# A convolution and deformable-sampling kernel: merged transfers on SyncE, and a denser table of taps and groups

## The chip, the cores and the metric

The kernel runs on one core of one Trainium2 chip. The metric is the device time of one execution in microseconds (us). The engines are TensorE (PE in the profile, PEld its weight loads), VectorE (DVE), ScalarE (ACT), GpSimd (POOL) and SyncE (SP), which here issues nearly all DMAs; 16 DMA engines move the bytes. Most executions agree within 0.3%.

## The reference, cut to what matters

```
x = x + _L0_conv_ref(_gn(x), ...)     # 14 convolutions and 2 upsamplings on (2, 64, 128, 128)
x = x + _L1_conv_ref(_gn(x), w_off, b_off, w_def)

offsets = conv3x3(x, w_off) + b_off   # 18 channels: dy, dx of 9 taps
val     = sum over 4 corners of x at (y + ky + dy, x + kx + dx), bilinear weights
out     = einsum('bckhw,ock->bohw', val, w_def)
```

The second line is a deformable convolution: for each pixel and each of nine taps it takes a value between pixels at a place that the offsets give, and weighs the values with a 64 x 64 matrix for each tap.

## The kernel before

**The stages.** Image 0 and then image 1 pass through the convolutions (until about 355 us and 737 us). After each, in the stage that I call *offsets*, TensorE computes the 18 offset channels, POOL splits them in three bfloat16 parts (`offp`), the normalised pixels are turned (`turned`), and SP stores both to DRAM: `store_parts` writes `offd`, one transfer for each of 8 tiles, `store_pixels` writes `pixd`. During image 0's offsets stage ACT's own queue loads image 1 into `xm`, and DVE takes its statistics as it comes. From about 780 us the *sampling* stage works on both images together, in 32 strips of four rows (`STRIPS`).

**A strip.** One strip needs windows of pixels (`win`, 12 transfers, `load_windows`), offsets (`offs`, for four strips at once, `load_offs`), and the first sum x1 (`x1t`, `load_x1`), and it stores its result (`store_strip`). All of them stand in SP's one queue, in this order for strip s: wait until all groups of s are sampled, load the windows of s+2, wait for the result of s, store it, load the x1 of s+2. After every fourth strip stands one `load_offs`.

**The units of a step.** In the step of strip s each engine goes through nine units, n = 0 to 8, always in program order. In unit n TensorE makes the distances of tap n of strip s+1 (`distances`, 8 matmuls, into one of two PSUM slots, so it needs the `absolute` of two units ago), ACT takes their absolute value (`absolute`), and DVE makes hat functions and products (`hats`, then `product` of the tap before). Behind that stand by tables:

- `WEIGHED_AT`: `weigh` of the last strip's taps on TensorE. The first of them waits until ACT has copied all six groups of that strip, with the two copies of columns at the edges that follow group 5.
- `GROUPS_AT`: `sample_group` on TensorE, a set of blocks of this strip (24 matmuls for groups 0 to 3 and 16 for 4 and 5, twice that in the trace since an f32 matmul stands there as two), and the copy of it out of PSUM, on ACT for groups 0, 1, 3, 4, 5 and on DVE for group 2. Group g uses the PSUM banks of group g-2, and waits for its copy.
- `RESULT_AT`: DVE adds the weighed sum and x1 (`strip_result`), before the `hats` of that unit. Group 1 uses the same banks as the sum, so it waits for this addition.

The waits that matter, in the code:

```
    if g >= 2:
        pe.wait_ge(*group_taken(s, g - 2))
...
        else:
            pe.wait_ge(strip_sum, s)
...
    pe.wait_ge(vals_act, (len(ACT_GROUPS) + 1) * (s + 1))
```

Strips 0 to 3 and the last four stand unrolled on TensorE; the others run in a loop.

Of the kernel before, what the change touches and what calls it, by code (L numbers as in the profile page):

```python
# [23 lines left out]
PS = 4  # L24
# [70 lines left out]
OFF_LOADS = 16 * 2 * PARTS * IMAGES  # L95
# [76 lines left out]
def build(nc, x, w4, w3, wds, wdec, woff, boff, wdef, wtaps, gmat, ident, sel, rampc, selg, places, out):  # L172
    es = ExitStack()
    with es:
# [233 lines left out]
        offd = nc.dram_tensor("offd", [IMAGES, ODD_AT, STRIPS + 2, PARTS * 2 * PS * HALF_W], BF16, kind="Internal").ap()  # L408
# [49 lines left out]
        def margins(eng):  # L458

            n = 0  # L460
            for b in range(IMAGES):
# [7 lines left out]
                for strip in (0, STRIPS + 1):  # L469
                    eng.dma_start(offd[b, 0:OFFC, strip, :], zeros_b[0:OFFC]).then_inc(pads_in, 16)  # L470
# [48 lines left out]
        def _(sp):  # L519
# [23 lines left out]
            def store_parts(b, n):  # L543

                sp.wait_ge(off_split, b * 8 + (n + 1 + SLOTS))
                batch, loc = divmod(n, 2)
                first = 1 + 8 * (2 * (batch // 2) + loc) + 4 * (batch % 2)
                dst = offd[bass.ds(b, 1), :, first:first + 4, :].rearrange("b c s n -> (b s) c n")
                sp.dma_start(dst, offp[:, n % SLOTS].rearrange("c p n -> c (p n)")).then_inc(parts_out[n % SLOTS], 16)
# [19 lines left out]
            def load_offs(q, slot):  # L569

                for b in range(IMAGES):
                    for h in range(2):
                        for part in range(PARTS):
                            lo = (2 * part + h) * PS * HALF_W
                            src = offd[b, 0:OFFC, bass.ds(QUAD * q, QUAD + 2), lo:lo + PS * HALF_W]
                            at = CH * h + OFFC * part
                            dst = offs[at:at + OFFC, slot, b].rearrange("c (s n) -> c s n", s=QUAD + 2)
                            sp.dma_start(dst, src).then_inc(offs_in[slot], 16)
# [12 lines left out]
            def strip_rows(d, t, j, two):  # L591

                return d[:, :, bass.ds(2 * PS * t + (PS * j + 2 * two - 1), 2), :].rearrange("b c i w -> b c (i w)")

            def load_x1(t, j):

                for two in range(2):
                    for b in range(IMAGES):
                        dst = x1t[CH * two:CH * two + CH, j, b]
                        if isinstance(t, int) and t == 0 and j == 0 and two == 0:  # L600
                            first = x1d[b, :, 0, :]
                            src = bass.AP(first.tensor, first.offset, [[H0 * W0, CH], [0, 2], [1, W0]])
                            sp.dma_start(dst.rearrange("c (i w) -> c i w", w=W0), src).then_inc(x1_in[j], 16)
                        else:
                            sp.dma_start(dst, strip_rows(x1d, t, j, two)[b]).then_inc(x1_in[j], 16)

            def store_strip(t, j):
                sp.wait_ge(strip_sum, 2 * t + (j + 1))
                for two in range(2):
                    for b in range(IMAGES):  # L610
                        src = outt[CH * two:CH * two + CH, j, b]
                        if isinstance(t, int) and t == 0 and j == 0 and two == 0:
                            sp.dma_start(out[b, :, 0, :], src[:, W0:2 * W0]).then_inc(out_done[j], 16)
                        else:
                            sp.dma_start(strip_rows(out, t, j, two)[b], src).then_inc(out_done[j], 16)
# [7 lines left out]
            def first_strips(b):  # L623
# [7 lines left out]
                for i in range(SLOTS):  # L631
                    sp.wait_ge(parts_out[i], MARGIN + (b * 32 + 16))
# [8 lines left out]
                load_offs(1, 1)  # L641

# [73 lines left out]
            for i in range(SLOTS):  # L716
                sp.wait_ge(pm_out[i], MARGIN + (IMAGES * 2 * 64))
                sp.wait_ge(parts_out[i], MARGIN + (IMAGES * 2 * 16))
# [7 lines left out]

            for j in range(2):
                load_x1(0, j)
# [16 lines left out]
            with sp.Fori(0, STRIPS // 8 - 1) as h:  # L745
                load_offs(2 * h + 2, 0)
                strip_pair(4 * h + 2)
# [1391 lines left out]
```

## Time and profile before

| | us |
|---|---|
| median of 3 runs | 1370.67 (1370.42 to 1372.49) |
| the profiled execution, its own time | 1373.18 |
| its span, first to last instruction | 1371.4 |

| engine | busy us, share of the span |
|---|---|
| PE | 1072.0, 78% |
| DVE | 886.0, 65% |
| ACT | 668.6, 49% |
| POOL | 62.2, 5% |

A load of x1 (64 KB) lands 2.2 us after its issue (median, the page's list of DMA issues).

The profile does not count the issuing of DMAs as busy, so SP has no line there: its queue is read in the timeline. Shares are means over stages with different limits.

### The profile page before, as it was taken

The page shows a single profiled execution, that of the slowest core. Times are in us where ns is not written, and L with a number is a line of the kernel's source. Part 1 is how long each engine was busy: PE and PEld are TensorE (multiplying, and loading weights), DVE is VectorE, ACT ScalarE, POOL GpSimd, SP SyncE. Part 2 cuts the span into 40 slices and gives each one's busy share as a digit, 9 for nine tenths or more (in the row PEclk, how much of TensorE's full clock was granted, in tenths as well). Part 3 has the DMA queues.
Part 4 walks back from the last instruction along what each step waited for, and adds up shares of the span by engine and source line. Part 5 has one row for each costly group of instructions (what it writes and reads, how often), then busy time and mean ns, then how long its engine had stood idle before and what let it go on. Part 6 is the DMA issues. An engine that isn't in the chain of part 4 may idle for free.

```text
span 1371.4 us, 42739 instructions
## 1 busy us (share of the span) xinstructions
PE 1072.0 (78%) x17334; PEld 675.1 (49%) x17334; DVE 886.0 (65%) x1379; ACT 668.6 (49%) x901; POOL 62.2 (5%) x87
## 2 busy tenths in 40 slices
PE   0799999975836999999767675888786878687875
PEld 0243346752312333467533254677565666566664
DVE  4878751527938777624279475888676867686870
ACT  0533433003444324330033774887776867586871
POOL 0000000000240000000002600000000000000000
PEclk9999999998877999999998778999999999898998
DMA  9000022204570000222034453433333333333341
GB/s 187 1 1 2 2 89 64 64 2 115 122 204 24 1 1 1 89 63 64 2 83 102 127 136 105 118 109 108 112 106 101 107 108 109 92 111 106 110 117 41
DMA packets 94709, 109.87 MB, mean 80 GB/s; under 512 B 12607, under 2 KB 81855, under 8 KB 92856
## 3 DMA queue, kind: packets, MB, share of 16 engines
q1 hardware_dynamic: 86056, 101.74, 27.6%
q10 hardware_dynamic: 8464, 5.37, 1.7%
q8 instruction: 147, 2.41, 0.8%
q14 instruction: 42, 0.34, 0.1%
HBM read 74.85 MB, written 32.22 MB: 78 GB/s over the span
## 4 chain that ended last, share of the span: by engine, by line
issue 47%; PE 38%; DVE 5%; ACT 3%; DMA 2%; POOL 2%; SPq 1%; ACTq 0%; POOLq 0%; DVEq 0%
PE psum L838 21%; PE psum L907 12%; DMA xm<-x 2%; PE psum L971 2%; DVE v L1632 1%; PE psum L948 1%; SPq L528 1%; POOL offr L2009 1%; POOL offp L2013 1%; ACT xm L1383 1%; PE psum L929 1%; DVE xm L1798 1%; PE psum L938 1%; DVE stats L1801 0%; PE psum L985 0%
## 5 line engine op out<-in xcount | busy, mean ns | idle before, releaser
L838 PE MATMUL psum<-v,u 64*64 64x512 f32 x3072 | 337.9, 597 | 17.9 <-DVE v L1632 12.7
L1455 ACT ACTIVATE dist<-psum 128x1024 f32<-128x1024 f32 x288 | 288.9, 1025 | 53.3 <-PE psum L1034 43.7
L1845 DVE TENSOR_SCALAR dist<-dist 128x1024 f32<-128x1024 f32 x288 | 198.2, 689 | 120.3 <-ACT dist L1455 119.7
L1081 PE MATMUL psum<-hat,win 64*64 64x144 f32 x4096 | 207.6, 332 | 86.7 <-DMA win<-pixd 45.5
L838 PEld LDWEIGHTS psum<-v,u 64*64 64x64 f32 x3072 | 133.3, 134 | 220.9 <-issue 220.5
L1081 PEld LDWEIGHTS psum<-hat,win 64*64 64x64 f32 x4096 | 160.3, 145 | 121.0 <-issue 119.0
L1855 DVE TENSOR_TENSOR hat<-dist 128x512 f32<-128x512 f32 x288 | 194.4, 684 | 0.3
L1458 ACT ACTIVATE val<-psum 128x864 f32<-128x864 f32 (+3 forms) x230 | 146.9, 676 | 94.8 <-PE psum L1081 87.1
L1154 PE MATMUL psum<-val,wdefs 64*64 64x256 f32 x1944 | 164.7, 394 | 32.5 <-ACT val L1458 24.2
L1034 PE MATMUL psum<-offs,sels 61*64 61x256 bf16 x2304 | 138.8, 287 | 19.7 <-issue 11.7
L1154 PEld LDWEIGHTS psum<-val,wdefs 64*64 64x64 f32 x1944 | 91.5, 137 | 46.3 <-issue 42.9
L1034 PEld LDWEIGHTS psum<-offs,sels 61*64 61x64 bf16 x2304 | 91.5, 113 | 34.4 <-issue 31.9
L1632 DVE TENSOR_TENSOR v<-stage 128x1024 f32<-128x1024 f32 x64 | 75.1, 1220 | 20.7 <-ACT stage L1334 20.7
L971 PE MATMUL psum<-tm,woffs 64*32 64x512 f32 x1152 | 70.4, 628 | 11.8 <-DVE tm L1749 11.8
L1632 DVE TENSOR_TENSOR v<-xm 128x1024 f32<-128x1024 f32 (+1 forms) x64 | 73.6, 1221 | 5.7 <-ACT xm L1342 4.1
L1325 ACT ACTIVATE mid<-psum 128x1024 f32<-128x1024 f32 x32 | 32.7, 1022 | 86.4 <-PE psum L838 86.4
L1342 ACT ACTIVATE xm<-xm 128x2048 f32<-128x2048 f32 x16 | 30.8, 1922 | 82.7 <-DVE xm L1682 82.7
L955 PE MATMUL psum<-gn,gmats 128*128 128x1 f32 x16 | 4.7, 362 | 80.2 <-DVE gn L1592 77.4
L1672 DVE TENSOR_TENSOR psum<-mid,psum 128x1024 f32<-128x1024 f32 x32 | 39.6, 1237 | 42.0 <-ACT mid L1325 42.0
L907 PE MATMUL psum<-htm,w3s 64*64 64x256 f32 x1152 | 63.0, 375 | 0.0
L1573 DVE SCALAR_TENSOR_TENSOR hxm<-psum,hxm 128x256 f32<-128x256 f32 x32 | 13.6, 424 | 73.7 <-PE psum L907 73.4
L1334 ACT ACTIVATE stage<-psum 128x1024 f32<-128x1024 f32 x32 | 36.4, 1143 | 47.0 <-PE psum L838 47.0
(144 smaller groups left out, 1094.8 us busy)
## 6 DMA issues: line engine op xcount, KB each, us to landing
win<-pixd SPq DMA_DIRECT2D x256, 68.0 KB
win<-pixd SPq DMA_DIRECT2D x128, 136.0 KB
raw<-x SPq DMA_DIRECT2D x16, 512.0 KB, 7.6
x1d<-xm SPq DMA_DIRECT2D x16, 512.0 KB, 6.0
pixd<-turned SPq DMA_DIRECT2D x64, 128.0 KB, 5.0
x1t<-x1d SPq DMA_DIRECT2D x128, 64.0 KB, 2.2
out<-outt SPq DMA_DIRECT2D x126, 64.0 KB, 2.1
offd<-offp SPq DMA_DIRECT2D x16, 384.0 KB
```

Source lines behind the costliest of these rows:

```text
L838: mm = pe.matmul(o, u4[half, i, v, ky, :], V[half, at:at + CHUNK, cg, v, :], start=start, stop=stop, skip_group_check=True)
L907: mm = pe.matmul(by_rows(o, level), w3s[CH * rg:CH * rg + CH, W_AT[layer], tap, :], rows_in(src, level, stride, rg, slot, step, tap), star ...
L971: mm = pe.matmul(by_rows(o, FULL), woffs[CH * rg:CH * rg + CH, tap, :], rows_in(T, FULL, 1, rg, slot, 4 * half + j, tap), start=tap == 0, ...
L1034: mm = pe.matmul(dst, sels[of, 2 * n + axis, :], offs[of, slot, b, lo:lo + PS * HALF_W], start=True, stop=True, skip_group_check=True)
L1081: mm = pe.matmul(dst[:, :, :, q:q + PS], win[half, j, b, block_ + h, :], rows, start=True, stop=True, skip_group_check=True)
L1154: mm = pe.matmul(dst.rearrange("c (r w) -> c r w", w=W0), w, val[half, slot, r0:r0 + 2, cols], start=k == 0, stop=k == TAPS - 1, skip_grou ...
L1455: act.activation(dist_at(j, n), psum[:, slot:slot + 2, :], ACT.Abs).then_inc(dist_abs, 1)
L1458: return act.activation(dst, src, ACT.Copy)
L1632: dve.tensor_tensor(dst, a, c, op).then_inc(v_made[v], 1)
L1672: dve.tensor_tensor(pair_banks(n, True), m2, m3, ALU.subtract).then_inc(minus_made, 1)
L1845: dve.tensor_scalar(d, d, 1.0, 1.0, ALU.min, ALU.subtract).then_inc(hats_made, 1)
L1855: dve.tensor_tensor(to, d[:, :, 0:PS * HALF_W], d[:, :, PS * HALF_W:], ALU.mult).then_inc(prod_dve, 1)
```

## The change

1. `offd` is laid out with the part as a dimension of its own. `store_parts` writes a tile in three transfers (one for each part) where it wrote one; `load_offs` reads all three parts at once: 4 transfers where there were 12. The constant `sel` has its rows in the new order.
2. `load_x1` and `store_strip` move both images in one transfer: two each for a strip where there were four.
3. The x1 of strips 0 and 1 is loaded inside `first_strips`, before the last pixels are stored, and no longer at the start of the strip loop.
4. The tables: taps in units 0 to 2, three each; groups 0 to 5 in units 3 to 8, one each; the result in unit 3.

```
-WEIGHED_AT = {1: [0, 1], 2: [2, 3], 3: [4, 5], 4: [6, 7, 8]}
-GROUPS_AT = {5: [0], 6: [1, 2], 7: [3], 8: [4, 5]}
-RESULT_AT = 5
+WEIGHED_AT = {0: [0, 1, 2], 1: [3, 4, 5], 2: [6, 7, 8]}
+GROUPS_AT = {3: [0], 4: [1], 5: [2], 6: [3], 7: [4], 8: [5]}
+RESULT_AT = 3
...
-                sp.dma_start(dst, offp[:, n % SLOTS].rearrange("c p n -> c (p n)")).then_inc(parts_out[n % SLOTS], 16)
+                for part in range(PARTS):
+                    dst = offd[bass.ds(b, 1), :, part, first:first + 4, :].rearrange("b c s n -> (b s) c n")
+                    sp.dma_start(dst, offp[:, n % SLOTS, part]).then_inc(parts_out[n % SLOTS], 16)
...
-                        for part in range(PARTS):
-                            lo = (2 * part + h) * PS * HALF_W
-                            src = offd[b, 0:OFFC, bass.ds(QUAD * q, QUAD + 2), lo:lo + PS * HALF_W]
+                        src = offd[b, 0:OFFC, :, bass.ds(QUAD * q, QUAD + 2), PS * HALF_W * h:PS * HALF_W * (h + 1)]
+                        dst = offs[CH * h:CH * h + HALF_K, slot, b].rearrange("c (s n) -> c s n", s=QUAD + 2)
+                        sp.dma_start(dst, src.rearrange("c p s n -> (c p) s n")).then_inc(offs_in[slot], 16)
...
+                        sp.dma_start(dst, strip_rows(x1d, t, j, two)).then_inc(x1_in[j], 16)
...
+                        sp.dma_start(strip_rows(out, t, j, two), src).then_inc(out_done[j], 16)
...
                 load_offs(1, 1)
+                for j in range(2):
+                    load_x1(0, j)
```

How the instructions stand on three engines, before and now (a row names its line, the operation, what it writes and reads, and the shape; line numbers shift by six):

TensorE, the later part of one step of the loop, before. `psum<-offs,sels` are distances, `psum<-val,wdefs` taps (here 7 and 8, with the last of 6), `psum<-hat,win` groups:

```order
L1034 MATMUL psum<-offs,sels 64x256 x8
L1154 MATMUL psum<-val,wdefs 64x256 x12
L1034 MATMUL psum<-offs,sels 64x256 x8
L1081 MATMUL psum<-hat,win 64x36x4 x12
L1034 MATMUL psum<-offs,sels 64x256 x8
L1081 MATMUL psum<-hat,win 64x36x4 x24
L1034 MATMUL psum<-offs,sels 64x256 x8
L1081 MATMUL psum<-hat,win 64x36x4 x12
L1034 MATMUL psum<-offs,sels 64x256 x8
L1081 MATMUL psum<-hat,win 64x36x4 x16
L1093 MATMUL psum<-hat,win 64x12 x8
```

The same place now:

```order
L1148 MATMUL psum<-val,wdefs 64x256 x12
L1028 MATMUL psum<-offs,sels 64x256 x8
L1075 MATMUL psum<-hat,win 64x36x4 x12
L1028 MATMUL psum<-offs,sels 64x256 x8
L1075 MATMUL psum<-hat,win 64x36x4 x12
L1028 MATMUL psum<-offs,sels 64x256 x8
L1075 MATMUL psum<-hat,win 64x36x4 x12
L1028 MATMUL psum<-offs,sels 64x256 x8
L1075 MATMUL psum<-hat,win 64x36x4 x12
L1028 MATMUL psum<-offs,sels 64x256 x8
L1075 MATMUL psum<-hat,win 64x36x4 x8
L1028 MATMUL psum<-offs,sels 64x256 x8
```

A group now stands between each two distances, where groups 1 and 2 (x24) and groups 4 and 5 (x16) stood together; group 2 follows the distances of unit 5, not of unit 6, and the taps stand in front of three distances, not of four.

DVE, from the result to the copy of group 2, before (`dist<-dist` is `hats`, `hat<-dist` is `product`, the rows of registers are waits):

```order
L1881 TENSOR_TENSOR outt<-psum,x1t 128x512
L1843 REGISTER_ALU
L1845 TENSOR_SCALAR dist<-dist 128x1024
L1855 TENSOR_TENSOR hat<-dist 128x512
L1843 REGISTER_ALU
L1845 TENSOR_SCALAR dist<-dist 128x1024
L1855 TENSOR_TENSOR hat<-dist 128x512
L1873 REGISTER_ALU
L501 COPY val<-psum 128x2x36x12
```

The same two now:

```order
L1875 TENSOR_TENSOR outt<-psum,x1t 128x512
L1837 REGISTER_ALU
L1839 TENSOR_SCALAR dist<-dist 128x1024
L1849 TENSOR_TENSOR hat<-dist 128x512
L1837 REGISTER_ALU
L1839 TENSOR_SCALAR dist<-dist 128x1024
L1849 TENSOR_TENSOR hat<-dist 128x512
L1837 REGISTER_ALU
L1839 TENSOR_SCALAR dist<-dist 128x1024
L1849 TENSOR_TENSOR hat<-dist 128x512
L1867 REGISTER_ALU
L502 COPY val<-psum 128x2x36x12
```

The result stands two units earlier, the copy one unit earlier, so three units of hats and products lie between them where two did.

SP, from the second load of offsets to the strip loop, before:

```order
L578 DMA offs<-offd 18x6x256 x12
L560 DMA pixd<-turned 16x8x256 x8
L549 DMA offd<-offp 4x32x1536
L560 DMA pixd<-turned 16x8x256 x4
L549 DMA offd<-offp 4x32x1536
L560 DMA pixd<-turned 16x8x256 x4
L549 DMA offd<-offp 4x32x1536 x2
L603 DMA x1t<-x1d 64x2x128 x2
L605 DMA x1t<-x1d 64x256 x6
```

The same place now:

```order
L577 DMA offs<-offd 54x6x256 x4
L601 DMA x1t<-x1d 64x2x128 x2
L603 DMA x1t<-x1d 64x2x256 x3
L562 DMA pixd<-turned 16x8x256 x8
L551 DMA offd<-offp 4x32x512 x3
L562 DMA pixd<-turned 16x8x256 x4
L551 DMA offd<-offp 4x32x512 x3
L562 DMA pixd<-turned 16x8x256 x4
L551 DMA offd<-offp 4x32x512 x6
```

The loads of x1 have moved in front of the last stores of pixels and parts, and each store of parts is three.

## Rows read from the trace of the kernel before

**Rows 1.** Waits of TensorE, 859 to 1332 us: total us, times, longest
```profile
PE psum L1081 <- DMA win<-pixd: 45.5, 13, 10.1
```

**Rows 2.** Waits of SP's queue, the same stretch
```profile
SPq L589 <- PE psum L1081: 0.8, 1, 0.8
```

**Rows 3.** Timeline of SP: start us, us, what, how many
```profile
817.73 1.17 SPq L549 DMA_DIRECT2D offd<-offp  x2
831.30 1.40 SPq L603 DMA_DIRECT2D x1t<-x1d  x2
...
836.67 7.82 SPq L589 DMA_DIRECT2D win<-pixd  x12
...
892.22 6.10 SPq L578 DMA_DIRECT2D offs<-offd  x12
...
966.50 9.14 SPq L589 DMA_DIRECT2D win<-pixd  x12
975.75 2.49 SPq L615 DMA_DIRECT2D out<-outt  x4
978.44 3.13 SPq L605 DMA_DIRECT2D x1t<-x1d  x4
...
1031.58 6.96 SPq L578 DMA_DIRECT2D offs<-offd  x12
```

**Rows 4.** Issues of the x1 loads, ns min/median/max
```profile
L605 SPq DMA_DIRECT2D x1t<-x1d x126: 468/532/1736, 832.7 to 1337.6; - x126
...
L603 SPq DMA_DIRECT2D x1t<-x1d x2: 659/672/686, 831.3 to 832.0; - x2
```

**Rows 5.** Timeline of ACT: start, us, in brackets idle before
```profile
873.47 1.05 ACT L1458 ACTIVATE val<-psum 128x576 f32<-128x576 f32 x3
...
885.99 0.97 ACT L1458 ACTIVATE val<-psum 128x864 f32<-128x864 f32 x1 [0.15 <-PE psum L1081]
886.84 1.02 ACT L1455 ACTIVATE dist<-psum 128x1024 f32<-128x1024 f32 x1
887.74 1.66 ACT L1458 ACTIVATE val<-psum 128x576 f32<-128x576 f32 x4
...
1330.68 1.64 ACT L1458 ACTIVATE val<-psum 128x576 f32<-128x576 f32 x4
```

**Rows 6.** Timeline of TensorE in the same strip, and two later places
```profile
878.48 1.51 PE L1154 MATMUL psum<-val,wdefs 64*64 64x256 f32 x23
879.72 0.49 PE L1034 MATMUL psum<-offs,sels 61*64 61x256 bf16 x7
879.94 0.31 PE L1081 MATMUL psum<-hat,win 64*64 64x144 f32 x1
...
885.91 0.84 PE L1081 MATMUL psum<-hat,win 64*64 64x144 f32 x16
...
889.69 1.09 PE L1154 MATMUL psum<-val,wdefs 64*64 64x256 f32 x16 [0.24 <-ACT val L1458]
...
926.63 1.28 PE L1081 MATMUL psum<-hat,win 64*64 64x144 f32 x23 [2.00 <-DMA win<-pixd]
...
1006.04 1.96 PE L1154 MATMUL psum<-val,wdefs 64*64 64x256 f32 x16
```

**Rows 7.** Timeline of DVE in the same strip: the result, the copy of group 2
```profile
881.64 0.68 DVE L1881 TENSOR_TENSOR outt<-psum,x1t 128x512 f32<-128x512 f32 x1
...
884.65 1.05 DVE L501 COPY val<-psum 128x864 f32<-128x864 f32 x1
```

**Rows 8.** Waits of TensorE, 820 to 837 us
```profile
PE psum L1081 <- DVE outt L1881: 16.2, 1, 16.2
```

**Rows 9.** Stretches: PE, PEld, DVE, ACT, POOL busy, PE clock, DMA share, GB/s
```profile
820.00:830.00 10.00, 0.30 (x11) 0.03 (x2) 0.14 (x1) 2.01 (x3) 0.00 (x0) 0.78 0.25 89
...
928.02:931.43 3.41, 3.41 (x65) 3.38 (x60) 1.39 (x3) 2.77 (x3) 0.00 (x0) 0.50 0.31 78
```

**Rows 10.** Timeline of DVE at image 1's start: its last statistics
```profile
412.51 2.48 DVE L1812 BATCH_NORM_STATS2 stats<-xm 128x6 f32<-128x512 f32 x4 [10.45 <-DMA xm<-x]
```

More of the change, by code:

```diff
@@ L94 @@
 LAST_BANKS = (4, 5)
[L95 removed]
+OFF_LOADS = 16 * 2 * IMAGES
 HALF_STRIP = BANK // 2
@@ L469, in margins @@
                 for strip in (0, STRIPS + 1):
-                    eng.dma_start(offd[b, 0:OFFC, strip, :], zeros_b[0:OFFC]).then_inc(pads_in, 16)
+                    eng.dma_start(offd[b, 0:OFFC, :, strip, :], zeros_b[0:OFFC].rearrange("c (p n) -> c p n", n=BANK)
+                                  ).then_inc(pads_in, 16)
         def settled(eng):
@@ L591, in strip_rows @@
             def strip_rows(d, t, j, two):
-                return d[:, :, bass.ds(2 * PS * t + (PS * j + 2 * two - 1), 2), :].rearrange("b c i w -> b c (i w)")
+                return d[:, :, bass.ds(2 * PS * t + (PS * j + 2 * two - 1), 2), :].rearrange("b c i w -> c b (i w)")
             def load_x1(t, j):
                 for two in range(2):
[L598 to L605, printed above, removed]
+                    dst = x1t[CH * two:CH * two + CH, j]
+                    if isinstance(t, int) and t == 0 and j == 0 and two == 0:
+                        for i in range(2):
+                            first = x1d[:, :, 0, :].rearrange("b c w -> c b w")
+                            sp.dma_start(dst[:, :, W0 * i:W0 * (i + 1)], first).then_inc(x1_in[j], 16)
+                    else:
+                        sp.dma_start(dst, strip_rows(x1d, t, j, two)).then_inc(x1_in[j], 16)
             def store_strip(t, j):
@@ L609, in store_strip @@
                 for two in range(2):
[L610 to L615, printed above, removed]
+                    src = outt[CH * two:CH * two + CH, j]
+                    if isinstance(t, int) and t == 0 and j == 0 and two == 0:
+                        first = out[:, :, 0, :].rearrange("b c w -> c b w")
+                        sp.dma_start(first, src[:, :, W0:2 * W0]).then_inc(out_done[j], 16)
+                    else:
+                        sp.dma_start(strip_rows(out, t, j, two), src).then_inc(out_done[j], 16)
             def sampling_constants():
@@ L725, in _ @@
             sp.wait_ge(off_split, IMAGES * 8 + SLOTS)
-            for j in range(2):
-                load_x1(0, j)
             def strip_pair(t, more=True):
@@ L745, in _ @@
             with sp.Fori(0, STRIPS // 8 - 1) as h:
-                load_offs(2 * h + 2, 0)
-                strip_pair(4 * h + 2)
-                strip_pair(4 * h + 3)
-                load_offs(2 * h + 3, 1)
-                strip_pair(4 * h + 4)
-                strip_pair(4 * h + 5)
+                for slot in range(2):
+                    load_offs(2 * h + (2 + slot), slot)
+                    strip_pair(4 * h + (2 + 2 * slot))
+                    strip_pair(4 * h + (3 + 2 * slot))
             strip_pair(STRIPS // 2 - 2)
@@ L767, in g_unit @@
                     for h in range(2):
-                        lo = (2 * part + h) * PS * HALF_W
-                        src = offd[bass.ds(b, 1), 0:OFFC, bass.ds(2 * t + (opar + 1), 1), lo:lo + PS * HALF_W]
+                        src = offd[bass.ds(b, 1), 0:OFFC, part, bass.ds(2 * t + (opar + 1), 1), PS * HALF_W * h:PS * HALF_W * (h + 1)]
                         dst = g_offs[OFFC * part:OFFC * part + OFFC].rearrange("c (r h x) -> c r h x", h=2, x=HALF_W)[:, :, h, :]
@@ L1878, in strip_result @@
                 dve.wait_ge(strip_conv, 4 * (s + 1))
-                dve.wait_ge(x1_in[j], uses * 64)
-                dve.wait_ge(out_done[j], MARGIN + ((uses - 1) * 64))
+                dve.wait_ge(x1_in[j], uses * 32 + 16 * (1 - j))
+                dve.wait_ge(out_done[j], MARGIN + ((uses - 1) * 32))
                 dve.tensor_tensor(outt[:, j], psum[:, SUM_BANKS[0]:SUM_BANKS[1] + 1, 0:HALF_STRIP], x1t[:, j],
@@ L2038, in selectors @@
         for part in range(PARTS):
-            s[:, OFFC * part + 2 * k + 1, k, 0] = 1.0
-            s[:, OFFC * part + 2 * k, k, 1] = 1.0
+            s[:, PARTS * (2 * k + 1) + part, k, 0] = 1.0
+            s[:, PARTS * 2 * k + part, k, 1] = 1.0
         s[:, HALF_K + 1 + K + kx, k, 0] = 1.0
```

20 lines of the change are left out of this document (8 added, 12 removed).

## The prediction

> **What bounds the kernel now.** I read the busy shares first: no engine is full, so something makes them wait, and the question is what ends the wait in each stage. The change touches the offsets stages lightly and the sampling stage in each of its 32 steps, so I read the waits there. TensorE waits 45.5 us in 13 waits for windows [rows 1], and the other engines' waits hang on those. The windows are late because of the queue that issues them: SP waited for TensorE only 0.8 us in 473 us [rows 2]. It issues without a pause: 9.1 us for the windows, 2.5 for four stores, 3.1 for four x1 loads, and 6 to 7 for the twelve offset loads after every fourth strip [rows 3]. From one load of offsets at 892.22 to the second next at 1031.58 are 8 strips in 139.4 us, 17.4 each.
>
> Strip by strip the end of the last copies on ACT is the best mark (I call it T). It stands at 874.52 for strip 3 (873.47 + 1.05), at 889.40 for strip 4 (887.74 + 1.66) and at 1332.32 for strip 30 [rows 5]. Strip 4, in which no window was late, took 14.9; the 27 steps to strip 30 took 16.96 each. So some 2 us of a step are SP's.
>
> **Part 1, SP per strip.** Two stores and two x1 loads fall away, and 8 offset loads of 12. What a merged transfer costs to issue no row shows exactly. The nearest is the first x1 load: it carries two runs for each of 64 partitions and took 0.67 where the plain one took 0.53 [rows 4]. From below a merged one costs what one costs now (0.53), from above what both cost (1.06). I take 0.67, as its shape is nearest. Then stores and loads take 4 x (0.67 + 0.1 between two) = 3.1 where they took 5.6: 2.5 saved; the offsets 4 x 0.7 for 6.5, 0.9 a strip. SP falls from 17.4 to 14.0, at the lower end 13.4, at the upper 17.
>
> The Trainium skill (Perfetto Trace Analysis, DMA Instruction — HWDGE) says that the issue as profiled holds the making of all descriptors. By it a merged transfer could cost what both did, the upper end. The rows do not fit a plain proportion: double the runs cost 0.67 against 0.53.
>
> **Part 2, the step on the engines.** If SP needs 14.0 and the engines more, the engines set the step, and now by the new tables. I follow the chain from T, with these spacings: ACT goes on 0.90 after an absolute value, 0.85 after a copy of 864 columns and 0.6 after one of 576, and the last group with its edge copies takes 1.06 (887.74 + 0.6 to 889.40) [rows 5]; three taps take 1.30 and a block of distances 0.22 before the next can start, and its ACT work starts 0.5 after it; 16 group matmuls are done after 0.84, so 24 after about 1.15; taps start 0.3 after T [rows 6]. On DVE five instructions lie between 881.64 and 884.65, so 0.60 each, and group 2's copy is 1.05 [rows 7]. In us after T:
>
> - Taps 0 to 2 run from 0.3 to 1.6, then distances 1, absolute 1 at 2.1; taps 3 to 5, distances 2 at 3.1, absolute 2 at 3.6; taps 6 to 8, distances 3 at 4.65, absolute 3 at 5.15. Absolute 0 had stood ready since T. So ACT idles 2.6 here: three taps and distances (1.5) stand against one absolute (0.9) in each unit. Before, five absolutes stood beside the same taps.
> - DVE: hats 2 at 4.7 (when absolute 2 ends), product 1 at 5.3, result 5.9 to 6.6. Group 1 can only then be sampled, from 6.75. ACT copies group 0 at 6.1, absolute 4 at 6.95, group 1 at 7.95, absolute 5 at 8.8, absolute 6 at 9.7, group 3 at 10.6, absolute 7 at 11.5.
> - DVE again: hats 5 has to wait for absolute 5 (ends 9.85), product 4 at 10.5, copy of group 2 from 11.1 to 12.1. Group 4 uses its banks, and starts 0.2 later, as at 884.65 + 1.05 and 885.91: 12.3. **This is what is late next**: ACT is free at 12.35 but gets group 4 at 13.2, absolute 8 at 13.8, group 5 at 14.7, T at 15.8.
>
> The old tables by the same chain give 14.5, and 14.9 was measured for strip 4; I add the difference, 0.35. So the step becomes **16.15**: 0.8 less than the mean of 16.96, though 1.25 more than a step of the old order that no window holds up. I keep 15.5 (nothing added, a little slack that I overlook) and 16.9 for the range. Over 27 steps: 27 x 0.81 = **21.9 us** less.
>
> Windows for strip s+2 are asked for at the end of step s and needed 4.9 into step s+2: 21 us, against 9.1 of issue and about 2.4 to land. They stay hidden while SP's 14.0 is below the step, so the two units by which group 0 moves ahead cost nothing. The store waits for the result, now 6.6 after T, still inside the 9.1 of the windows ahead of it.
>
> **Part 3, the start of sampling.** Now strip 1's group 1 waits 16.2 us [rows 8]: the result of strip 0 wants x1, whose loads stand behind the last stores' landing and are issued at 831.30 [rows 3]. With the loads moved ahead this wait goes. What is late next is the windows of strip 2: SP waits until all parts have landed before the strip loop, and only then issues them. They were issued at 836.67, after 5.4 us of x1 loads; now right behind the landing. But the landing moves. While only parts move, 10 us long, the DMA share is 0.25 with 89 GB/s [rows 9]: four engines of 16. A store of parts (393 KB) costs them 4.4 us, the four last ones 17.7. Pieces of 1 KB where they were 3 KB make this dearer, I take 15% (0 to 40%), +2.7. SP reaches the stores about 0.8 earlier (8 offset loads fewer at 0.5, five x1 loads more at 0.67), and issues 8 more transfers of 0.58 [rows 3], hidden behind the four engines' backlog. The landing goes from 831.3 to 833, group 0 of strip 2 is sampled at 833 + 7.8 + 2.4 = 843.2, T of strip 2 is 10.9 later (15.8 - 4.9), and T of strip 3 at 870.3 or with a slow clock at first 870.7, against 874.5: **3.8 us** less. Of the 16.2 only this is left.
>
> The Trainium skill (DMA: Bandwidth & Descriptors, the section on a DMA's increment of 16) has the number of engines as the largest divisor up to 16 of both sides' outermost sizes, and the lowest-numbered ones. The outermost size is 4 before and after, so by it the three transfers share the same four engines; were it otherwise, this landing would come some 8 us earlier.
>
> **Part 4, between the images.** Image 1's last statistics wait 10.45 us for its load [rows 10], which ACT's queue had issued some 20 us before and which shares those four engines with the parts. Two things change: eight stores take 1.2 us more of SP each and 15% more of the four engines (later, up to +4), and a piece of x of 512 bytes waits behind pieces of 1 KB, not of 3 KB, where the two queues take turns (earlier, up to -10). No row tells which weighs more. I take **-4**.
>
> **Part 5, the rest.** The last strip and the closing 39 us stay, within 1.
>
> **Sum.** 1373.18 (the profiled execution's own time, 2.5 over the median) - 21.9 - 3.8 - 4 = 1343.5, less 2.5: **1341 us**.
>
> **The rivals.**
>
> - *The clock falls in the new gaps* (slower). TensorE now idles about 1.8 twice in a step: before group 4 and before the taps, with 2 us of work between. For it: after a gap of 2.00 that ends at 926.63 [rows 6] the clock stood at 0.5, its lower level of 1.2 GHz, from 928.02 for 3.4 us [rows 9]; against it: before strip 4's taps 1.1 us did nothing. At that level 16 tap matmuls took 1.96 where they took 1.09 [rows 6], so a low stretch on the taps costs 1.7 a step; in each step that is 27 x 1.7 = 46, and 1341 + 46 = 1387. It decides from 17.2 a step on, two steps in three.
> - *The engines are not as far behind as the chain says*: the step comes down to the 14.9 of strip 4. 27 x 2.06 = 56 in place of 21.9: 1307. For it: the load of each unit is more even than before; against it: two waits of the chain (1.50 for each absolute beside three taps, group 2's copy) follow from program order.
> - *SP gets no shorter*, since a merged transfer costs what its parts did (the upper end): steps of 16.9, and only 3.8 and 4 are won: 1363. Were the start not won either, 1371, no change.
>
> **How the numbers follow.** The forecast 0.60 (1321 to 1360 with steps of 15.5 to 16.7 and the parts 3 and 4 at their ends); the clock 0.14; 14.9 a step 0.15; SP 0.11. A measurement of this kernel can tell 0.2% (2.7 us) from no change. Faster: 0.57 of the forecast's 0.60, the 0.15, and 0.09 of SP's: 0.81. Same: 0.02 + 0.02 + 0.01 = 0.05. Slower: the rest, 0.14. The range reaches over SP's case and part of the clock's above, and about to the third case below: 1308 to 1374.
>
> **What would show it.** In the profile after: SP's timeline with pauses in front of the windows of each strip; TensorE no longer waiting for windows; ACT waiting about 1 us for group 4 in each step, and TensorE at group 4 for DVE's copy of group 2; T every 16.15 us; the first x1 load before the last pixels, no wait of 16 us at strip 1 but some 10 at strip 2 for windows. The prediction is wrong if SP still issues without a pause, if the clock reads 0.5 in most steps, or if TensorE's gap at group 4 is missing.

## The result, and the profile after

| | before | after |
|---|---|---|
| median, us | 1370.55 (1369.78 to 1372.49) | 1333.49 (1329.97 to 1339.16) |
| profiled execution, us | 1373.18 | 1329.97 |
| its span, us | 1371.4 | 1328.2 |
| mean TensorE clock | 0.927 | 0.950 |

The ratio is 0.9731, with an interval of 0.9695 to 0.9768: 37 us less. Forecast were 1341, between 1308 and 1374. Of all executions in this document one, the slowest of e11 (1329.27 us, clock 0.907), ran in a slower state and is left out of e11's time. The total is close; its terms are not, as a count along the span shows. The count compares the two profiled executions, which differ by 43.2 us and not 37: that of before lies 2.6 above its median, and that of after is the fastest of its four. T is again the end of a strip's last copies on ACT, read as in [rows 5].

| stretch of the span | before | after | less | forecast |
|---|---|---|---|---|
| start to the first pixel store of image 1 | 737.37 | 725.44 | 11.9 | 4 |
| from there to T of strip 3 | 137.15 | 123.06 | 14.1 | 3.8 |
| T of strip 3 to T of strip 30, 27 steps | 457.80 | 440.45 | 17.35 | 21.9 |
| from there to the end | 39.1 | 39.25 | -0.2 | 0 |

So the steps gave 4.6 us less than forecast and the two stretches ahead of them 18 us more: that the total came within 8 us of the forecast is in part luck.

The first view is the waits over the steps, 850 to 1290 us, TensorE and then SP's queue (in total us, times, the longest):
```profile
PE psum L1075 <- DVE val L502: 48.6, 27, 1.8
PE psum L1148 <- ACT val L1452: 34.6, 21, 1.8
PE psum L1075 <- DVE outt L1875: 14.5, 27, 0.6
PE psum L1028 <- issue: 9.8, 4, 4.6
```
```profile
SPq L588 <- PE psum L1087: 54.3, 22, 4.0
```
The line that stood first before, the wait for windows [rows 1], is gone, and SP now waits for TensorE (54.3 us) where it waited 0.8 us [rows 2]. What TensorE waits for instead is, 27 times in 27 steps, DVE's copy of group 2, as forecast. The fourth line was not in the forecast.

SP's timeline around strip 4 and at the start of sampling:
```profile
778.61 1.48 SPq L601 DMA_DIRECT2D x1t<-x1d  x2
...
782.08 5.16 SPq L562 DMA_DIRECT2D pixd<-turned  x8
...
797.67 5.11 SPq L551 DMA_DIRECT2D offd<-offp  x6
809.92 7.80 SPq L588 DMA_DIRECT2D win<-pixd  x12
...
858.57 2.15 SPq L577 DMA_DIRECT2D offs<-offd  x4
863.07 9.11 SPq L588 DMA_DIRECT2D win<-pixd  x12
872.40 1.58 SPq L613 DMA_DIRECT2D out<-outt  x2
874.17 1.52 SPq L603 DMA_DIRECT2D x1t<-x1d  x2
878.85 9.02 SPq L588 DMA_DIRECT2D win<-pixd  x12
```
Two merged stores take 1.58 and two merged loads 1.52, against 2.49 and 3.13 for four each [rows 3]. SP is done at 875.69 and pauses until 878.85. And x1 of the first strips now goes out ahead of the last pixels (778.61).

One step, from T of strip 3 (847.44 + 1.06 = 848.50) to T of strip 4 (863.39 + 1.07 = 864.46), on ACT, with the last strip of the count (1287.89 + 1.06 = 1288.95):
```profile
847.44 1.06 ACT L1452 ACTIVATE val<-psum 128x576 f32<-128x576 f32 x3
848.83 1.02 ACT L1449 ACTIVATE dist<-psum 128x1024 f32<-128x1024 f32 x1 [0.33 <-issue]
850.76 1.02 ACT L1449 ACTIVATE dist<-psum 128x1024 f32<-128x1024 f32 x1 [0.91 <-PE psum L1028]
...
861.89 0.74 ACT L1452 ACTIVATE val<-psum 128x576 f32<-128x576 f32 x1 [0.67 <-PE psum L1075]
...
863.39 1.07 ACT L1452 ACTIVATE val<-psum 128x576 f32<-128x576 f32 x3
...
1287.89 1.06 ACT L1452 ACTIVATE val<-psum 128x576 f32<-128x576 f32 x3
```
ACT has its gap beside the taps (0.91) and its gap in front of group 4 (0.67).

TensorE in the same step, and at strip 12:
```profile
860.99 0.83 PE L1075 MATMUL psum<-hat,win 64*64 64x144 f32 x16 [1.83 <-DVE val L502]
...
864.76 1.53 PE L1148 MATMUL psum<-val,wdefs 64*64 64x256 f32 x24 [1.68 <-ACT val L1452]
...
978.78 0.64 PE L1028 MATMUL psum<-offs,sels 61*64 61x256 bf16 x8 [4.65 <-issue]
979.37 2.84 PE L1148 MATMUL psum<-val,wdefs 64*64 64x256 f32 x24
```
(The rows count an f32 matmul twice: groups 0 to 3 are 12 matmuls in the program and 24 in a row, groups 4 and 5 are 8 and 16.) The two gaps are there, 1.83 and 1.68, and the clock does not fall in them: over the 120 us from 850 to 970 it is 1.00. But at strip 12, and again at strip 20, TensorE stands still for 4.65 and 4.46 us with nothing to wait for; behind the stop its clock is at 0.5 (24 taps in 2.84 for 1.53), and the step takes 21.56 and 21.46. Both places are the back edge of TensorE's loop (the jump from its end to its start), which runs three times over eight strips. Of the 27 steps 23 lie between 15.7 and 16.3.

The DVE timeline at image 1's start and the stretches in which parts leave (columns as in [rows 9]):
```profile
384.57 4.85 DVE L1806 BATCH_NORM_STATS2 stats<-xm 128x6 f32<-128x512 f32 x8 [5.74 <-issue]
...
401.01 2.47 DVE L1806 BATCH_NORM_STATS2 stats<-xm 128x6 f32<-128x512 f32 x4 [6.50 <-DMA xm<-x]
```
```profile
412.00:418.00 6.00, 5.01 (x24) 1.44 (x28) 6.00 (x6) 5.95 (x6) 0.00 (x0) 0.53 0.27 93
803.00:808.00 5.00, 4.51 (x110) 4.26 (x108) 3.60 (x6) 3.47 (x5) 0.00 (x0) 0.96 0.28 99
```
The last statistics start at 401.01 where they started at 412.51 [rows 10]. The parts still go out at about a quarter of the 16 engines (0.27 and 0.28), and at 93 and 99 GB/s are no slower than the 89 of [rows 9].

### The profile page after: what moved, and what is told of

Read it like the earlier page. It is cut to its first block, busy times and chain, and to the rows that moved or that the text cites. A ratio compares the mean times of both kernels' runs of the same rounds, so it can differ in the third digit from the quotient of the medians.

```text
span 1328.2 us, 42328 instructions
## 1 busy us (share of the span) xinstructions
PE 1041.4 (78%) x17334; PEld 681.5 (51%) x17334; DVE 890.0 (67%) x1379; ACT 665.3 (50%) x901; POOL 61.5 (5%) x87
## 4 chain that ended last, share of the span: by engine, by line
issue 46%; PE 40%; DVE 5%; ACT 2%; POOL 2%; DMA 2%; SPq 1%; POOLq 0%; DVEq 0%; ACTq 0%
PE psum L832 22%; PE psum L901 12%; PE psum L965 3%; DMA xm<-x 2%; DVE v L1626 1%; PE psum L942 1%; SPq L529 1%; POOL offp L2007 1%; POOL offr L2003 1%; ACT xm L1377 1%; PE psum L979 1%; PE psum L923 1%; DVE xm L1792 1%; PE psum L932 1%; DVE stats L1795 0%
## 5 line engine op out<-in xcount | busy, mean ns | idle before, releaser
L832 PE MATMUL psum<-v,u 64*64 64x512 f32 x3072 | 335.4, 595 | 17.5 <-DVE v L1626 12.7
L1449 ACT ACTIVATE dist<-psum 128x1024 f32<-128x1024 f32 x288 | 292.5, 1031 | 85.8 <-PE psum L1028 77.4
L1839 DVE TENSOR_SCALAR dist<-dist 128x1024 f32<-128x1024 f32 x288 | 202.1, 702 | 105.3 <-ACT dist L1449 105.3
L1075 PE MATMUL psum<-hat,win 64*64 64x144 f32 x4096 | 202.7, 317 | 76.2 <-DVE val L502 55.6
L832 PEld LDWEIGHTS psum<-v,u 64*64 64x64 f32 x3072 | 144.0, 134 | 207.4 <-issue 199.1
L1075 PEld LDWEIGHTS psum<-hat,win 64*64 64x64 f32 x4096 | 152.9, 135 | 95.5 <-issue 93.4
L1148 PE MATMUL psum<-val,wdefs 64*64 64x256 f32 x1944 | 157.1, 396 | 45.9 <-ACT val L1452 37.2
L1452 ACT ACTIVATE val<-psum 128x864 f32<-128x864 f32 (+3 forms) x230 | 151.6, 678 | 37.4 <-PE psum L1075 29.8
L1028 PEld LDWEIGHTS psum<-offs,sels 61*64 61x64 bf16 x2304 | 92.8, 111 | 28.7 <-issue 23.8
```

The source lines that it names most:

```text
L832: mm = pe.matmul(o, u4[half, i, v, ky, :], V[half, at:at + CHUNK, cg, v, :], start=start, stop=stop, skip_group_check=True)
L1028: mm = pe.matmul(dst, sels[of, 2 * n + axis, :], offs[of, slot, b, lo:lo + PS * HALF_W], start=True, stop=True, skip_group_check=True)
L1075: mm = pe.matmul(dst[:, :, :, q:q + PS], win[half, j, b, block_ + h, :], rows, start=True, stop=True, skip_group_check=True)
L1148: mm = pe.matmul(dst.rearrange("c (r w) -> c r w", w=W0), w, val[half, slot, r0:r0 + 2, cols], start=k == 0, stop=k == TAPS - 1, skip_grou ...
L1449: act.activation(dist_at(j, n), psum[:, slot:slot + 2, :], ACT.Abs).then_inc(dist_abs, 1)
L1452: return act.activation(dst, src, ACT.Copy)
```

## The experiments

All are the changed kernel with the thing that is named made different (two things in e9, e11 and e12), except e2, which is the kernel before with the new tables. Step is (T of strip 30 - T of strip 3) / 27 of the profiled execution.

| run | median, us | ratio to before, interval | T of strip 3 | step |
|---|---|---|---|---|
| before | 1370.55 | 1 | 874.52 | 16.96 |
| after | 1333.49 | 0.9731 (0.9695 to 0.9768) | 848.50 | 16.31 |
| e1 old tables | 1302.38 | 0.9488 (0.9444 to 0.9531) | 850.73 | 15.14 |
| e2 new tables alone | 1379.39 | 1.0038 (1.0013 to 1.0063) | 876.11 | 17.02 |
| e3 one store of parts | 1339.01 | 0.9746 (0.9699 to 0.9792) | 862.72 | 16.12 |
| e4 old layout of parts | 1353.54 | 0.9847 (0.9799 to 0.9895) | 874.75 | 16.21 |
| e5 group 2 early | 1356.67 | 0.9872 (0.9825 to 0.9918) | 855.33 | 17.05 |
| e6 groups 1, 2 and 4, 5 | 1311.31 | 0.9546 (0.9498 to 0.9594) | 850.62 | 15.49 |
| e7 x1 late | 1333.92 | 0.9713 (0.9682 to 0.9744) | 852.87 | 16.18 |
| e8 x1 and results unmerged | 1337.95 | 0.9741 (0.9696 to 0.9785) | 858.35 | 16.19 |
| e9 old tables, result 4 | 1298.15 | 0.9465 (0.9418 to 0.9512) | 852.22 | 14.92 |
| e10 straight TensorE | 1323.59 | 0.9612 (0.9571 to 0.9654) | 857.93 | 15.79 |
| e11 result 4, straight | 1313.14 | 0.9592 (0.9527 to 0.9657) | 851.24 | 15.39 |
| e12 old tables, unmerged | 1328.76 | 0.9675 (0.9645 to 0.9704) | 849.34 | 15.95 |

The ratios are to executions of the kernel before taken beside each set of runs, whose medians were 1372.87 (e1, e3, e4, e5), 1374.29 (e2, e6, e8, e9) and 1373.46 (e7, e10, e11, e12). The changed kernel was not taken again beside them. So a difference of two medians from different sets is good to some 5 us: e10 is 10 us under the changed kernel by the medians and 16 by the ratios, e1 31 and 33.

**e1: the old tables under the new transfers.**
```diff
-WEIGHED_AT = {0: [0, 1, 2], 1: [3, 4, 5], 2: [6, 7, 8]}
-GROUPS_AT = {3: [0], 4: [1], 5: [2], 6: [3], 7: [4], 8: [5]}
-RESULT_AT = 3
+WEIGHED_AT = {1: [0, 1], 2: [2, 3], 3: [4, 5], 4: [6, 7, 8]}
+GROUPS_AT = {5: [0], 6: [1, 2], 7: [3], 8: [4, 5]}
+RESULT_AT = 5
```


> The changed kernel with the old tables (taps in units 1 to 4, groups in 5 to 8, result in 5); the transfers stay merged. Theory (the merged transfers win, the new tables lose on the engines): a step takes 14.5 to 14.9 us where it takes 15.8, 27 steps, so about 28 us less than the changed kernel's 1333: 1305 (1300 to 1312), and SP, at 13.3 a strip, still pauses in front of the windows. Rival (the new tables win by themselves): 1340 or more. Second rival (SP binds again as soon as the engines are faster): steps of 15.5 and waits for windows, 1325.


It took 1302.38, as the theory had it and 31 us less than the changed kernel, and the step fell by 1.17, 27 times: 31.6. So the new tables lose 31 us and the rest of the change, the transfers and their order, wins some 70. SP still has time to spare (waits 850 to 1260 us):
```profile
SPq L588 <- PE psum L1087: 29.5, 17, 4.4
```

**e2: the new tables alone**, the same three lines put into the kernel before.

> The kernel before with the three new tables and nothing else: 12 loads of offsets in every fourth strip, four stores and four loads of x1 in each. Theory (SP sets the step of the kernel before at 17.0 to 17.4, and the new tables' own chain of 15.8 is shorter than that): the time stays near 1371, between 1368 and 1383, with TensorE still waiting for windows. The statistics and the start stay as before. Rival (the new tables are the gain): 1340 or less. Second rival (TensorE's clock falls in the new gaps when the windows are late as well): steps of 17.7, 1390.


1379.39, 0.4% slower than the kernel before beside it (1374.29), within the theory's range. SP's queue and TensorE, 876 to 1336 us:
```profile
SPq L589 <- PE psum L1081: 0.5, 1, 0.5
```
```profile
PE psum L1081 <- DVE val L501: 46.4, 27, 1.9
...
PE psum L1081 <- DMA win<-pixd: 15.6, 4, 4.2
```
SP never rests, and windows come late (15.6 us) although the engines' chain is longer. With SP as the bound the longer chain of the new tables costs 0.06 a step (17.02 for 16.96): the two bounds do not add.

**e3: one store for each tile of parts, new layout.**
```diff
-                for part in range(PARTS):
-                    dst = offd[bass.ds(b, 1), :, part, first:first + 4, :].rearrange("b c s n -> (b s) c n")
-                    sp.dma_start(dst, offp[:, n % SLOTS, part]).then_inc(parts_out[n % SLOTS], 16)
+                dst = offd[bass.ds(b, 1), :, :, first:first + 4, :].rearrange("b c p s n -> (b s) c p n")
+                sp.dma_start(dst, offp[:, n % SLOTS]).then_inc(parts_out[n % SLOTS], 16)
```


> The changed kernel with each tile of parts stored by one transfer again, in the new layout, so in pieces of 1 KB still. Theory (image 1 loads sooner since the pieces in front of its own on the four engines are short): DVE's last statistics of image 1 start at about 401 us as in the changed kernel, and the time stays within 4 us of 1333. Rival (three transfers are what frees the engines): they start at about 410, and the time is 8 to 15 us more.


1339.01, 5.5 us over the changed kernel with intervals that overlap: between the theory and the rival. The last statistics start at 404.42, so the sooner loading of image 1 does not hang on the number of stores.

**e4: the old layout**: pieces of 3 KB, one store for each tile, twelve loads of offsets; x1, results and tables as changed.
```diff
-        offd = nc.dram_tensor("offd", [IMAGES, ODD_AT, PARTS, STRIPS + 2, BANK], BF16, kind="Internal").ap()
+        offd = nc.dram_tensor("offd", [IMAGES, ODD_AT, STRIPS + 2, PARTS * 2 * PS * HALF_W], BF16, kind="Internal").ap()
```


> The changed kernel with the old layout of the parts in DRAM: stored by one transfer in pieces of 3 KB, and loaded by 12 transfers for four strips; x1, results and tables as in the change. Theory (piece size): the last statistics of image 1 start at about 412, 11 us later, the parts land 5 to 9 us later before the strip loop, and SP has 0.9 us a strip more, which it can spare: 1352 (1346 to 1358). Rival (the layout does not matter, SP's count of transfers does): the statistics stay at 401 and the time within 1333 to 1340.


1353.54, in the theory's range. e3 and e4 together separate the layout from the number of stores (the offset loads, in which they differ too, stand outside the two stretches compared here). Statistics on DVE, first of e3, then of e4:
```profile
386.94 4.85 DVE L1805 BATCH_NORM_STATS2 stats<-xm 128x6 f32<-128x512 f32 x8 [5.87 <-issue]
...
404.42 1.88 DVE L1805 BATCH_NORM_STATS2 stats<-xm 128x6 f32<-128x512 f32 x3 [6.83 <-DMA xm<-x]
```
```profile
384.87 4.86 DVE L1810 BATCH_NORM_STATS2 stats<-xm 128x6 f32<-128x512 f32 x8 [6.01 <-issue]
...
413.29 2.48 DVE L1810 BATCH_NORM_STATS2 stats<-xm 128x6 f32<-128x512 f32 x4 [10.55 <-DMA xm<-x]
```
From the first to the start of the last four are 28.4 us with the old layout (e4), 17.5 with the new one in one store (e3), 16.4 in three (after): of the 12.0 us between e4 and the changed kernel the layout, with its pieces of 1 KB, gives 10.9. The other traces bear it out: 26.2 to 28.7 in the three with the old layout (before, e2, e4), 15.8 to 18.8 in the ten with the new one in three stores.

At the other place, the landing of image 1's parts, it is the number of stores that tells. From SP's first pixel store of that group to the first windows behind the landing (SP's timelines, first e3, then e4; after has 782.08 to 809.92):
```profile
788.85 6.83 SPq L561 DMA_DIRECT2D pixd<-turned  x8
...
822.27 7.95 SPq L587 DMA_DIRECT2D win<-pixd  x12
```
```profile
805.62 6.09 SPq L560 DMA_DIRECT2D pixd<-turned  x8
...
836.77 7.85 SPq L589 DMA_DIRECT2D win<-pixd  x12
```
That is 31.15 us in e4, 33.42 in e3 and 27.84 in after: small pieces in one store are 2.3 dearer, three stores instead of one 5.6 cheaper. The same stretch takes 31.1 to 32.0 in the three traces with the old layout and 27.8 to 29.3 in the ten with three stores; e3 is one trace, so its two differences are good to about 1.5 us. Where the windows were issued 25.6 us after T of strip 0 (e4), TensorE waited for them at strip 2 for the time that the prediction's rule gives, and where it was 18.0 (e3) for 2.4:
```profile
PE psum L1079 <- DMA win<-pixd: 10.2, 1, 10.2
```

**e5: group 2 one unit earlier**, so that DVE's copy is done in time for group 4.
```diff
-GROUPS_AT = {3: [0], 4: [1], 5: [2], 6: [3], 7: [4], 8: [5]}
+GROUPS_AT = {3: [0], 4: [1, 2], 6: [3], 7: [4], 8: [5]}
```


> The changed kernel with group 2 sampled and copied in unit 4 and no longer in unit 5, all else as in the change. Theory (DVE's late copy of group 2 holds group 4 up): the wait of TensorE for that copy goes, the step falls from 15.8 to 15.15, 27 x 0.65 = 18 us less: 1315 (1311 to 1321). Rival (only the taps in front of the distances set the step, the copy's wait would be filled by another one at once): within 4 us of 1333.


The opposite came: 1356.67, with most steps at 16.8 to 17.1. TensorE at strip 5, and two stretches:
```profile
872.68 2.84 PE L1148 MATMUL psum<-val,wdefs 64*64 64x256 f32 x24 [2.20 <-ACT val L1452]
```
```profile
868.00:870.20 2.20, 1.76 (x57) 1.32 (x52) 2.02 (x4) 2.20 (x4) 0.00 (x0) 1.00 0.58 173
872.51:875.92 3.41, 3.24 (x37) 2.31 (x41) 1.49 (x3) 0.77 (x1) 0.00 (x0) 0.50 0.46 138
```
The wait for DVE's copy was gone, and strip 3, where a gap of 2.19 left the clock at 1.00, took the 15.20 that the chain gives. But the gap ahead of the taps had grown from 1.68 to 2.2, in nearly all steps behind it the clock fell, and 24 taps took 2.84 instead of 1.53. From 855 to 970 us the mean clock is 0.90, where the changed kernel has 1.00. The theory for this run fell on the prediction's own slower rival.

**e6: short gap and early groups together.**
```diff
-GROUPS_AT = {3: [0], 4: [1], 5: [2], 6: [3], 7: [4], 8: [5]}
+GROUPS_AT = {3: [0], 4: [1, 2], 6: [3], 7: [4, 5]}
```


> The changed kernel with groups 1 and 2 behind unit 4 and groups 4 and 5 behind unit 7 (units 5 and 8 have none). Theory (a step is the chain of program order; TensorE's clock falls in a step only where its gap ahead of the taps passes about 2 us): by the chain the step is 14.3 and the gap ahead of the taps 1.0, so the clock stays at 1.0 and the time falls to about 1295 (1290 to 1305), 1.5 us less for each of 27 steps. Rival (moving group 2 ahead is what hurt in the run with group 2 at unit 4 alone, whatever the gap): 1350 or more, with the clock at 0.5 in most steps.


1311.31, 22 us less than the changed kernel though 16 over what was expected. TensorE, 850 to 1270 us:
```profile
PE psum L1148 <- ACT val L1452: 24.3, 22, 1.3
```
The gaps ahead of the taps are 1.1, and group 2 stands as early as in e5: the early group by itself did not cost e5 its clock. 13 of the 27 steps take 14.3 to 14.8, as the chain says; two hold a loop edge (20.0 and 19.5), and the others take 15 to 17. In five of these (strips 9, 11, 17, 28 and 30, 16.0 to 17.0 us) the mean clock of the step is 0.89 or 0.90, though no gap of TensorE in them is longer than 1.13. So the length of the gap ahead of the taps is not all that decides on the clock; why it fell there nothing here settles.

**e7: x1 of strips 0 and 1 behind the landing**, as before.
```diff
-                for j in range(2):
-                    load_x1(0, j)
...
+            for j in range(2):
+                load_x1(0, j)
```


> The changed kernel with one thing undone: the four loads of x1 for strips 0 and 1 are issued behind the landing of the last parts, as before, and no longer ahead of the last pixels. Theory (the wait of strip 1's group 1 comes back, counted from the earlier landing): the parts have landed at 809.2, x1 is issued until 812.6 and has landed about 815, where strip 0's last copies end at 799.4; T of strip 1 comes near 826 for 816.7, and all behind it 9 us later: 1342 to 1343. Rival (the wait never counted, only SP's order does): the windows of strip 2 come 2.8 later and the time is 1336. Second rival: within 2 us of the changed kernel.


1333.92, the second rival's result in the median. The trace shows why it is not nothing: SP reached the parts 3 us sooner, and issued x1 at 806.44 and the windows at 809.93, the same time as in the changed kernel. DVE stood 3.9 us in front of the result, until 810.7, while x1 landed:
```profile
L1876 DVE TENSOR_TENSOR outt<-psum,x1t x2: 683/687/691, 810.7 to 827.3; 128x512 f32<-128x512 f32 x2
its engine sat idle before it (us, times) until:
  issue: 3.9, 1
```
From T of strip 0 (796.76) to T of strip 3 (852.87) it took 56.1, the changed kernel 51.6 (796.93 to 848.50): 4.5 us, half the 9 expected, and as long as TensorE's one wait for that result. But e8 and e10, whose x1 is early, take 55.6 and 55.8 for the same stretch, with stops of TensorE that wait for nothing. The 27 steps gave 3.6 back in this execution, with shorter stops of TensorE's loop (steps of 18.9 and 20.0). What the move is worth by itself is below what the medians tell.

**e8: four loads of x1 and four stores of results**, parts and offsets merged.
```diff
-                    dst = x1t[CH * two:CH * two + CH, j]
+                    for b in range(IMAGES):
+                        dst = x1t[CH * two:CH * two + CH, j, b]
...
-                    src = outt[CH * two:CH * two + CH, j]
+                    for b in range(IMAGES):
+                        src = outt[CH * two:CH * two + CH, j, b]
```


> The changed kernel with four loads of x1 and four stores of results in each strip, as before, in place of two and two; the offset parts stay merged. Theory (SP needs 13.3 a strip after the change, merging these four saved 2.5, and the new tables' chain is 15.8): SP comes to 15.8 a strip, level with the chain, so 0 to 0.4 a step is lost: 1334 to 1346. Rival (these two merges carry the whole gain of the sampling stage): steps of 17 again, 1352 or more.


1337.95, as the theory had it. Between 858 and 1296 us SP does not wait for TensorE any more, yet TensorE does not wait for windows. SP's timeline:
```profile
1006.59 9.08 SPq L588 DMA_DIRECT2D win<-pixd  x12
1015.90 2.65 SPq L614 DMA_DIRECT2D out<-outt  x4
1018.75 3.55 SPq L604 DMA_DIRECT2D x1t<-x1d  x4
1022.59 9.03 SPq L588 DMA_DIRECT2D win<-pixd  x12
```
16.0 us for this strip, and 15.7 in the mean of three (the windows three strips on start at 1053.69), without offset loads: level with the engines.

**e12: the same with the old tables.**

> The changed kernel with the old tables and with four loads of x1 and four stores of results in each strip, as before; parts and offsets stay merged. Theory (these two merges are worth nothing under the new tables, whose chain of 15.8 is as long as SP's 15.7 without them, but they are what lets the old tables run at 14.8): SP's 15.7 to 16 set the step, about 1.1 more for each of 27 than in the run of the old tables, 1332 (1325 to 1338). Rival (SP does not bind at 15.7 either): 1302 to 1308.


1328.76, as the theory had it and 26 us over e1. So the merged x1 and results are worth 26 under the old tables; under the new ones the 4 of e8 are not clear of noise, since the intervals overlap. TensorE, 850 to 1280 us, waits for windows again (12.9 us, 11 times).

**e9: old tables, result one unit earlier.**
```diff
-RESULT_AT = 5
+RESULT_AT = 4
```


> The changed kernel with the old tables, as in the run of the old tables, but the result one unit sooner (behind unit 4 in place of 5). Theory (the chain of program order): DVE's result stands ahead of the hats of unit 4 and group 1 is free sooner, TensorE's gap of 1.0 in the middle of the step goes, the step is 13.9 for 14.5, but SP's 13.3 to 14 a strip is then close: 1285 to 1300, 1290 likeliest. Rival (SP or the windows' landing binds at 14.4 already): 1302, no change to the run of the old tables.


1298.15 is the lowest of all, but its interval overlaps e1's. TensorE's waits for the result, 15.8 us in e1 (23 times), are gone as expected, and the step came down 0.2 and not 0.6.

**e10: TensorE's loop written out.**
```diff
-            with pe.Fori(0, STRIPS // 8 - 1) as h:
+            for h in range(STRIPS // 8 - 1):
```


> The changed kernel, with TensorE's loop over the middle 24 strips (three passes of eight) written out as straight code, tables and all other engines as they are. Theory (the two steps of 21.5, at strips 12 and 20, are the back edges of TensorE's loop: gaps of 4.65 and 4.46 and a clock at 0.5 behind them): both gaps go, all steps are 15.8 to 16, and the time is 11 us less, 1322. Rival (the engine has to fetch as many instructions at that place whether it jumps or not, so straight code stops as long or elsewhere): 1333, or slower.


1323.59, 10 us less than the changed kernel. TensorE's waits, 850 to 1290 us, whole:
```profile
PE psum L1075 <- DVE val L502: 51.3, 28, 1.9
PE psum L1148 <- issue: 42.9, 28, 1.6
PE psum L1075 <- DVE outt L1875: 14.8, 27, 0.6
```
The stops of 4.65 and 4.46 are gone, and all 27 steps take 15.7 to 16.3, 15.79 in the mean. (The line with issue is the old gap ahead of the taps, 28 times, 1.5 in the mean, without a named releaser.) The steps give 14 us in this trace, but its T of strip 3 comes 9.4 us later than the changed kernel's, in code that the edit does not touch: among other things TensorE stops, waiting for nothing, for 2.2 us until 800.77 and 2.7 until 805.63.

**e11: the same on e9.**

> The best version so far (old tables, result behind unit 4, all transfers as changed), with TensorE's loop written out as well. Theory (back edges cost 3 us each here, steps of 17.7 and 17.9 among steps of 14.7): 6 us less than its run, about 1292 (1287 to 1296). Rival (straight code has to be fetched as well): 1298 or more.


Its rival held: 1313.14 (1308.82 to 1313.35), 15 over e9, with a step of 15.39 for 14.92. Where the loop had two long stops, TensorE now stops in the middle of runs that have nothing to wait for:
```profile
930.89 0.33 PE L1143 MATMUL psum<-val,wdefs 64*64 64x128 f32 x2
...
932.96 0.41 PE L1028 MATMUL psum<-offs,sels 61*64 61x256 bf16 x8 [1.71 <-issue]
```
In e10 such stops could hide in two gaps of 1.6 and 1.8 in each step, which e11's tables do not have. That is an argument from the two traces; no run shows the supply of instructions itself.

## Why the prediction was right, and where it was not

- **Part 1, SP**: right. A merged transfer was taken at 0.67; the pairs took 1.58 and 1.52, so about 0.7 each with the space between. SP has its pauses. e2 shows the other half: without this the step stays at 17. (The upper end was put too high: with 1.06 for each merged transfer the prediction's own terms save 1.0 a strip, so 16.4 and not 17.)
- **Part 2, the chain**: its later moments hold within 0.2 us. After T of strip 4 (864.46) the result was to start at 5.9 and did at 5.96, group 2's copy at 11.1 and did at 11.11; group 4 was to start 12.3 after T and did at 12.49 in strip 4 (860.99). DVE's rows:
```profile
870.42 0.69 DVE L1875 TENSOR_TENSOR outt<-psum,x1t 128x512 f32<-128x512 f32 x1
...
875.57 1.05 DVE L502 COPY val<-psum 128x864 f32<-128x864 f32 x1
```
  The chain gave 15.8, and the plain steps took 15.8. **One step that failed is "I add the difference, 0.35"**: the old order's missing 0.4 was no property of the new one. And the term was still too large a saving, 21.9 for 17.35. The second step that failed is what it was taken from: the 16.96 of before is a mean over all 27 steps, with the two back edges of TensorE's loop in it (stops of 3.66 and 3.22, steps of 18.9 and 18.7), and from it was taken a plain step without any. In the changed kernel the two edges cost 2 x 5.7 beyond a plain step. So 16.15 came near the measured 16.31 by luck: 0.35 without a cause stood where 0.51 of edges and a few long steps belonged. e10 takes the edges away and has 15.79.
- **Part 3, the start**: mis-sized, 3.8 for 14.1. The wait of 16.2 went [rows 8], and nothing took its place: TensorE does not wait for windows from 796 to 850 us, because the parts had landed some 10 us sooner, counted from T of strip 0, than the forecast had it (the windows behind the landing start 13.0 after that T; the forecast's landing at 833 is 22.9 after the 810.07 of before). Of the 9.9 us SP's sooner arrival at the stores gives 3.3 (the first pixel store stands 14.9 ahead of that T where it stood 10.7, and 0.8 was forecast) and the way from there to the landing 6.6 (27.85 for 31.95, where the forecast's 833 has 2.5 more). Two assumptions failed. "Pieces of 1 KB make this dearer, I take 15%, +2.7" was itself about right for one store (e3 over e4: +2.3), but three stores win about 5 (5.6 in after, 4.1 in the longest of the other traces). "8 offset loads fewer" forgot that the offsets are loaded twice ahead of the stores, so 16 are fewer. The rule for the late windows was right, but not reached: e4 and e3 show its waits, 10.2 and 2.4. And by e7, with the parts landed early, the x1 loads in their old place cost TensorE one wait of 4.5 where it was 16.2: most of what was won here is the landing and not the moved x1.
- **Part 4, between the images**: the sign and its source, the smaller pieces of the parts, were right, and the size was not, -11.9 for -4; the end of the range, -10, was nearest. e4 has 28.4 from first to last statistics where e3 has 17.5. How it comes about, that the two queues take turns at shared engines, was argued and not measured by itself.
- **The clock rival**: not in the changed kernel, where the gaps ahead of the taps are 1.7. But e5 puts them at 2.2 and pays the rival's price: 1.7 a step was named, and a step with the clock down takes 17.0 for 15.2. Between the two tables lies 0.5 us of gap; e6, where the clock fell in five steps with gaps of 1.1, shows that this is no margin to build on.
- **The rival of 14.9**: out. That step belongs to the old tables. The prediction said that the new order takes 1.25 more a step than the old where no window is late; e1 measures 1.17. It did not draw the conclusion that the tables were a loss, hidden behind the gain of the rest: transfers about -70, tables +31.
- **SP gets no shorter**: out, by SP's waits.

## What to carry to other kernels

When a change joins two things, forecast each of them alone on top of the other: here the tables cost next to nothing while SP was the bound (e2: +5) and 31 us once it was not. Follow a chain of program order in full and add no correction without a cause: it gave the plain steps of the changed kernel and of e10. It is about the least that a step takes here, and not more than that: in e5, e6 and e9 the clock, or stops that wait for nothing, made many steps longer. Count what stands outside a plain step, such as a loop's edges, at its own row, and compare plain steps with plain steps. A transfer's gain depends on the bound that stands next (26 us, or at most a few, for the same merge).

## What was not expected of the hardware

- The back edge of TensorE's loop over eight strips costs 3 to 6 us: in the changed kernel 4.65 and 4.46 us without a matmul, and a low clock behind; in e1 stops of 3.5 and 3.1. The Trainium skill (Advanced Engine Details and Errata, Control Flow Timing) gives a compare-and-branch about 108 ns, so it is not the branch itself. The same page (ISA Cache) gives TensorE 128 KB of instruction cache in lines of 256 instructions; that the loop's body does not stay there would fit e10 and e11, but no run here shows it. Nor are such stops bound to a back edge: in ten of the fourteen traces TensorE stops for 1.3 to 3.3 us, with nothing to wait for, within 5 us of T of strip 0, where no loop turns.
- Straight code is no free cure: it won 10 us with slack in each step (e10) and lost 15 without (e11).
- One store of 393 KB holds up what follows it more than three of 131 KB with the same pieces: 33.42 us to the landing in e3, 27.8 to 29.3 in the ten traces with three stores. The longest issue of a pixel store in that group is 2.6 to 2.9 us in the four traces with one store and 1.0 to 2.2 in the ten with three.
- The granted clock fell to 0.5 in nearly every step with one gap of 2.2 ahead of the taps (e5), in almost none with two of 1.7 and 1.8 (the changed kernel), and in five of the 25 steps without a loop edge with gaps of 1.1 (e6).
